# Score products of an attention block on row groups of 32: one head per group, both stacks double buffered

## The reference

```
a   = layernorm(x) @ w_attn + b_attn            # q, k, v; 16 heads of 8
s   = q @ k.T / sqrt(8) + slope[head] * key_position, causal
y   = softmax(s) @ v ;  x2 = x + y @ w_proj + b_proj
z   = layernorm(x2)
out = x2 + gate(z) * sum over 8 experts of (gelu(z @ w1 + b1) @ w2 + b2)
```

## Time and profile before

| | |
|---|---|
| median of three runs | 341.5 us |
| profiled execution, first to last instruction (span) | 341.4 us |
| PE busy | 295.9 us (87%), 1784 matrix instructions |
| PEld busy | 193.8 us (57%) |
| DVE busy | 192.6 us (56%) |
| ACT busy | 193.7 us (57%) |
| POOL busy | 84.1 us (25%) |
| chain that ended last, by engine | PE 74%, DVE 12%, DMA 7% |

### The profile page before, as it was taken

One profiled execution on the slowest core, in us unless ns is written; L12 is line 12 of the kernel. 1 busy time (PEld: TensorE's weight loads), 2 busy tenths in 40 slices (PEclk: granted clock), 3 DMA queues, 4 the chain that ended last, 5 costly groups with the idle time before them and its releaser, 6 DMA issues.

```text
span 341.4 us, 5507 instructions
## 1 busy us (share of the span) xinstructions
PE 295.9 (87%) x1784; PEld 193.8 (57%) x1784; DVE 192.6 (56%) x787; ACT 193.7 (57%) x322; POOL 84.1 (25%) x213
## 2 busy tenths in 40 slices
PE   0245899997979999699999997899999999998994
PEld 0133466565556676466766765557756665655661
DVE  5624759776786867145677776264867741161111
ACT  1871064463455568275759467376667788634462
POOL 8569203240233027002033126002210220000030
PEclk9985579999999999699999999899999999999999
DMA  7166500070120006200300028001100100000101
GB/s 198 66 90 96 193 2 2 16 122 9 38 74 4 0 19 105 29 2 18 95 1 4 0 61 120 3 2 44 35 4 2 35 2 2 0 2 0 31 1 31
DMA packets 12380, 13.29 MB, mean 39 GB/s; under 512 B 2048, under 2 KB 9088, under 8 KB 12096
## 3 DMA queue, kind: packets, MB, share of 16 engines
q1 hardware_dynamic: 11328, 11.90, 16.1%
q0 software_dynamic: 1024, 1.05, 1.9%
HBM read 5.21 MB, written 1.05 MB: 18 GB/s over the span
## 4 chain that ended last, share of the span: by engine, by line
PE 74%; DVE 12%; DMA 7%; issue 3%; ACT 1%; POOL 1%; DVEq 0%; SPq 0%; ACTq 0%; POOLq 0%
PE ffn_bank L835 16%; PE a_ring L742 11%; PE v_ring L720 11%; PE pv_bank L767 9%; DMA k_stack<-k_lo 6%; PE a_ring L673 5%; DVE unused L1047 5%; PE a_ring L748 5%; PE a_ring L674 4%; PE a_ring L675 4%; DVE xn L967 2%; PE v_ring L796 1%; PE v_ring L729 1%; DMA x_in<-x 1%; PE v_ring L673 1%
## 5 line engine op out<-in xcount | busy, mean ns | idle before, releaser
L1047 DVE CUSTOM_DVE_ANT_0 unused<-v_ring,cst 128x512 bf16<-128x512 f32 (+3 forms) x256 | 112.1, 487 | 68.5 <-PE v_ring L720 63.9
L553 ACT ACTIVATE probs<-a_ring 128x512 f32<-128x512 f32 (+1 forms) x192 | 92.5, 526 | 74.7 <-PE a_ring L748 73.5
L720 PE MATMUL v_ring<-k_stack,q_stack 128*128 128x512 f32 (+3 forms) x256 | 89.6, 422 | 20.2 <-DMA k_stack<-k_lo 15.3
L742 PE MATMUL a_ring<-q_stack,k_stack 128*128 128x512 f32 (+3 forms) x256 | 76.8, 360 | 0.4 <-DMA q_stack<-m_lo 0.4
L720 PEld LDWEIGHTS v_ring<-k_stack,q_stack 128*128 128x128 f32 x256 | 49.5, 210 | 40.6 <-issue 23.5
L570 ACT ACTIVATE hidden<-a_ring,cols_sb 128x512 f32<-128x512 f32 x64 | 43.4, 688 | 43.2 <-PE a_ring L675 42.7
L835 PE MATMUL ffn_bank<-hidden,w_sb 128*128 128x512 f32 x128 | 66.3, 602 | 1.1 <-ACT ffn_T L579 0.8
L742 PEld LDWEIGHTS a_ring<-q_stack,k_stack 128*128 128x128 f32 x256 | 46.7, 197 | 7.8 <-issue 4.0
L748 PE MATMUL a_ring<-score_mask,ident_bf 128*128 128x128 bf16 (+1 forms) x192 | 48.1, 252 | 0.0
L767 PE MATMUL pv_bank<-probs,v_ones 128*32 128x256 f32 (+3 forms) x512 | 43.2, 447 | 0.0
L673 PE MATMUL a_ring<-zT_hi,w_hi 128*128 128x512 f32 x64 | 34.2, 534 | 0.8 <-DVEq L953 0.8
(11 more groups left out here) (109 smaller groups left out, 298.4 us busy)
## 6 DMA issues: line engine op xcount, KB each, us to landing
q_stack<-q_hi SPq DMA_DIRECT2D x8, 256.0 KB
k_stack<-k_hi SPq DMA_DIRECT2D x64, 32.0 KB
x_in<-x SPq DMA_DIRECT2D x4, 256.0 KB, 3.6
hidden<-w SPq DMA_DIRECT2D x1, 1024.0 KB, 8.3
q_stack<-q_lo SPq DMA_DIRECT2D x4, 256.0 KB
k_stack<-k_lo POOLq DMA_DIRECT2D x32, 32.0 KB, 4.0
w_sb<-w SPq DMA_DIRECT2D x1, 1024.0 KB, 5.2
x_res<-x SPq DMA_DIRECT2D x4, 256.0 KB, 3.1
```

Of the source, the lines that this page charges most:

```text
L553: act.activation(probs[:, n % 2, q, KIND_AT[kind]:KIND_AT[kind] + cols], a_bank()[:, 0:cols], ACT.Exp).then_inc(e_freed, 1)
L720: last = pe.matmul(dst[:, at:at + P * (n + 1)], q_stack[b % 2][:, s, n * P:(n + 1) * P], k_stack[:, s, q, 0:P * (n + 1)], start=True, stop ...
L742: pe.matmul(dst[:, at:at + P * (TB - j)], k_stack[:, s, q, j * P:(j + 1) * P], q_stack[b % 2][:, s, j * P:T], start=(at == 0), stop=False, ...
L1047: ins = dve.tensor_tensor_reduce(unused[:, (uses[0] - 1) % V_BANKS, at:at + cols], bank_[:, at:at + cols], cst[:, C_MASK + T - cols:C_MASK ...
```

## The change

Each head gets 32 rows of its own, `QR * q` to `QR * q + 31`, in both stacks: 8 rows of q high (or k high), 8 of q low (k high), 8 of q high (k low), then two slope rows (24, 25), two maxima rows (26, 27), four unused. `k_stack` has no copies by head any more and is double buffered as `q_stack` is. A max unit reads 26 rows and an exp unit 28 rows at partition 32 q. The fill with zeros, the transfer of zeros, and POOL's transfers go away. Max units now go kind by kind like exp units, and exp units start with head 2, so that heads of neighbouring units differ. All loads of q and k are transfers of 64 KB from 32 partitions to 8, twelve for q and twelve for k per batch, issued by SP, for batch 0 the k ones by ACT. The mask product is unchanged.

```
+HEAD_D = 8
+ALIBI_ROWS, MAX_ROWS, STACK_ROWS = 24, 26, 28
...
-        k_stack = sb("k_stack", [P, SETS, QUADS, T], F32R)
+        k_stack = [sb(f"k_stack{i}", [P, SETS, T], F32R) for i in range(2)]
...
+        def send_term(queue, stack, term, part, loaded):
+            for q in range(QUADS):
+                row = QR * q + HEAD_D * term
+                queue.dma_start(stack[row:row + HEAD_D, :, :].bitcast(F32),
+                                part[QR * q:QR * (q + 1), :].bitcast(F32)).then_inc(loaded, 16)
+        def send_q(queue, b):
+            if b < 2:
+                queue.wait_ge(q_const, SETS * (b + 1))
+            else:
+                queue.wait_ge(e_filled, UNITS * SETS * (b - 1))
+            queue.wait_ge(q_split, 2 * b + 1)
+            send_term(queue, q_stack[b % 2], 0, q_hi, q_loaded)
+            send_term(queue, q_stack[b % 2], 2, q_hi, q_loaded)
+            queue.wait_ge(q_split, 2 * b + 2)
+            send_term(queue, q_stack[b % 2], 1, q_lo, q_loaded)
+        def send_k(queue, b):          # the same with k_const, k_split, k_hi (terms 0, 1), k_lo (term 2)
...
+        def exp_order(k):
+            return k // QUADS, (k + QUADS // 2) % QUADS
...
                     if s == 2 and b + 1 < B:
-                        load_k(b + 1, 0)
-                        load_q(b + 1)
+                        send_k(sp, b + 1)
+                        send_q(sp, b + 1)
...
-            pool.memset(k_stack[0:CONST_ROWS, 0:2, :, :].bitcast(F32), 0.0).then_inc(k_zeros, 1)
-            pool.memset(k_stack[0:CONST_ROWS, 2:4, :, :].bitcast(F32), 0.0).then_inc(k_zeros, 1)
-            load_k_low(0, 0)
-            load_k_low(0, 1)
...
             q_constants(0)
             k_constants(0)
             split_high(0, 1)
             split_high(0, 0)
+            send_k(act, 0)
             k_constants(1)
...
-                q, kind = k // KINDS, k % KINDS
+                kind, q = k // QUADS, k % QUADS
+                rows = slice(QR * q, QR * q + MAX_ROWS)
...
-                    last = pe.matmul(dst[:, at:at + P * (n + 1)], q_stack[b % 2][:, s, n * P:(n + 1) * P],
-                                     k_stack[:, s, q, 0:P * (n + 1)], start=True, stop=True)
+                    last = pe.matmul(dst[:, at:at + P * (n + 1)], q_stack[b % 2][rows, s, n * P:(n + 1) * P],
+                                     k_stack[b % 2][rows, s, 0:P * (n + 1)], start=True, stop=True)
...
+                rows = slice(QR * q, QR * q + STACK_ROWS)
-                    pe.matmul(dst[:, at:at + P * (TB - j)], k_stack[:, s, q, j * P:(j + 1) * P],
-                              q_stack[b % 2][:, s, j * P:T], start=(at == 0), stop=False, skip_group_check=True)
+                    pe.matmul(dst[:, at:at + P * (TB - j)], k_stack[b % 2][rows, s, j * P:(j + 1) * P],
+                              q_stack[b % 2][rows, s, j * P:T], start=(at == 0), stop=False, skip_group_check=True)
```

More of the change, by code:

```diff
@@ L38 @@
 QR = P // QUADS
-TERMS = 3
 MASKED = -3.0e38
@@ L319, in chunk @@
             return n // SETS, range(first, first + sizes[n % SETS])
[L321 to L325, removed]
+        def send_term(queue, stack, term, part, loaded):
[14 more added lines that the diff above has]
+        def send_k(queue, b):
+            if b < 2:
+                queue.wait_ge(k_const, SETS * (b + 1))
+            else:
+                queue.wait_ge(e_filled, UNITS * SETS * (b - 1))
+            queue.wait_ge(k_split, 2 * b + 1)
+            send_term(queue, k_stack[b % 2], 0, k_hi, k_loaded)
+            send_term(queue, k_stack[b % 2], 1, k_hi, k_loaded)
+            queue.wait_ge(k_split, 2 * b + 2)
+            send_term(queue, k_stack[b % 2], 2, k_lo, k_loaded)
+        def exp_order(k):
+            return k // QUADS, (k + QUADS // 2) % QUADS
         def inverse_sqrt(engine, settle, y, src, scale, eps, v, t, fused=False):
@@ L356, in load_residual @@
                 sp.dma_start(x_res[:], x_view[b]).then_inc(xres_loaded, 16)
[L358 to L380, removed]
             def load_max(b, s):
                 sp.wait_ge(m_ready, SETS * b + s + 1)
[L384 to L385 removed]
+                for r, part in ((MAX_ROWS, m_hi), (MAX_ROWS + 1, m_lo)):
+                    sp.dma_start(q_stack[b % 2][r::QR, s, :].bitcast(F32),
                                  part[:].bitcast(F32)).then_inc(m_loaded, 16)
@@ L433, in split_low @@
             def split_low(b, part):
-                full, hi, lo, parts, loads, count = (
-                    (k_full, k_hi, k_lo, k_split, k_low_loaded[0] + k_low_loaded[1], K_LOW_LOADS * b),
-                    (q_full, q_hi, q_lo, q_split, [q_loaded], q_count(b)))[part]
+                full, hi, lo, parts, loaded = ((k_full, k_hi, k_lo, k_split, k_loaded),
+                                               (q_full, q_hi, q_lo, q_split, q_loaded))[part]
                 pool.wait_ge(parts, 2 * b + 1)
                 if b >= 1:
-                    for loaded in loads:
-                        pool.wait_ge(loaded, count)
+                    pool.wait_ge(loaded, STACK_LOADS * b)
                 pool.tensor_tensor(lo[:], full[:], hi[:].bitcast(F32), ALU.subtract).then_inc(parts, 1)
@@ L447, in set_ones @@
                 pool.memset(slots[:, :, :, 16 + 8 * e:24 + 8 * e], 1.0).then_inc(v_const, 1)
-            def load_k_low(b, half):
-                if b == 0:
-                    pool.wait_ge(k_zeros, half + 1)
-                else:
-                    pool.wait_ge(e_filled, UNITS * (SETS * (b - 1) + 2 * half + 2))
-                pool.wait_ge(k_split, 2 * b + 2)
-                for q in range(QUADS):
-                    send_k(pool, k_lo, half, 1, q, k_low_loaded[half][q])
             steps = [0]
@@ L585, in split_high @@
             def split_high(b, part):
-                full, hi, ready, parts, loads, count = (
-                    (k_full, k_hi, k_ready, k_split, k_loaded[0] + k_loaded[1], K_LOADS * b),
-                    (q_full, q_hi, q_ready, q_split, [q_loaded], q_count(b)))[part]
+                full, hi, ready, parts, loaded = ((k_full, k_hi, k_ready, k_split, k_loaded),
+                                                  (q_full, q_hi, q_ready, q_split, q_loaded))[part]
                 act.wait_ge(ready, b + 1)
                 if b >= 1:
-                    for loaded in loads:
-                        act.wait_ge(loaded, count)
+                    act.wait_ge(loaded, STACK_LOADS * b)
                 act.activation(hi[:], full[:], ACT.Copy).then_inc(parts, 1)
```

77 lines of the change are left out of this document (28 added, 49 removed).

## The result

The changed kernel takes 433.1 us (median of five runs, 431.2 to 438.1) beside 341.5 (339.8 to 343.9) for the kernel before: a ratio of 1.267, 95% interval 1.260 to 1.275. The profiled execution is the longest of the five (438.1; the others had 431.2 to 433.2); its span of 436.3 us stands against 341.4.

The account below looks back on a forecast made before the run. It took PE's stream of products plus four waits for loads as the bound; 341.4 + 45 (stream) + 5 (start) - 3 (borders) = 388 us, range 338 to 400, likeliest case alone 378 to 400.

Parts of the forecast that it names:

- the granted clock falls: Rival on PE: emptier stretches bring its clock to 1.2 GHz for a good part, over 400 us; chance 0.04.
- Passing, forecast +3.0 a set: PE's stream: 13 tiled stretches per set pay for switching to and from whole-array products, 48 us for 16 sets.
- The price at pv: Read at the column-tiled pv products on PE: some 0.10 us in, 0.10 out, then first weights unhidden.
- The overlap: PE products of different heads running at the same time; alone, with free passing, worth 1.07 us per set, 17 in all.
- The first cycle: PE: max 384 + 128, exp 512, mask 128 take 0.81 us instead of 0.64, four times a set.
- the second pair: PE: max 256, exp 384 + 128, mask 256 take 0.77 us instead of 0.48, three times a set.
- The seven pairs: PE, per set: four max-exp pairs at +0.17 to +0.18 us each and three at +0.28.
- the other stretches: PE's remaining tiled stretches per set, exp units alone or other unit groupings, each +0.11 to +0.29 us.
- The upper bound of the stream, +65: PE's stream with the column form's passing price and no overlap: 48 + 17 = 65 us.
- The start, forecast +5: First max unit waits for all 24 transfers, landing at 34.5 us instead of 29.59; bounds +3 and +15.
- the bound made from it, 44: Start: at 0.25 us a packet the first loads would land at 44 us, the +15 bound.
- The borders, forecast -3: PE's load waits before set 3 at three batch borders: 4.3 and twice 0.7 us, against 2.8 + 3.1 + 3.2.

Follow-up runs that it names:

- spread: Changed kernel with its 24 transfers of 64 KB per batch going to 32 partitions instead of 8 (rows misplaced, for times only): 397.6 us, 1.159.
- loads_rows64: Kernel before with q and k loads reordered, max and exp products on rows 0 to 63 for every head (for times only): 425.2 us, 1.239.

## Why the prediction was wrong

The direction was right, and passing between tiled and whole-array products does cost time, as forecast. The time was 45 us over the forecast and 33 over the top of the range. The step that failed is the clock, which the sum left at nothing: it stood apart as the rival "the granted clock falls" with a chance of 0.04, where it was the largest term. The prices of the start and of the borders were too small as well; the price of the stream at full clock was too large, which hid part of it.

**The clock, forecast at nothing.** 40 to 50 us. It was set apart as a rival of its own, as if it excluded the forecast; it came on top of it. It was also looked for in the wrong place: "if emptier stretches bring it to its lower level". The stretches at the lower level are not empty (53.00 busy of 53.00 in spread). The row that was quoted, 0.82 from 40 to 60 us, comes from early sets that are score products nearly alone, with PE busy 18.92 of 20; there the clock had not fallen but not yet risen from the wait for the first loads (up at 47.1, PE at work from 29.59). The change takes four fifths of the rows from just those products, and what this does to the clock was never asked.

**Passing, forecast +3.0 a set: +1.8 measured, 29 us instead of 48.** The price at pv holds: 0.10 in and 0.10 out, against 0.22 for a tiled mask. Without overlap the prediction's own terms give 3.0 + 1.07 = 4.1, and loads_rows64 has 3.7. The overlap was taken too small. The first cycle was forecast at 0.81 us and takes 0.60. That a weight load does not wait for the other row group's is the likely reason. PE's weight loads after:

```profile
320.34 0.18 PEld L686 LDWEIGHTS v_ring<-k_stack,q_stack 26*128 26x128 f32 x1
320.34 0.29 PEld L709 LDWEIGHTS a_ring<-q_stack,k_stack 28*128 28x128 f32 x2
```

Two loads start together, where the prediction took them one after another at 0.107. For the second pair it forecast 0.77, and 0.64 is measured. The seven pairs were forecast at +1.5 a set and cost +0.3, which is the whole difference; the other stretches were forecast at +1.4 and cost some +1.5. The upper bound of the stream, +65, left the clock out and was passed (70.5).

**The start, forecast +5: +15.6.** The number of engines, eight, was right. The packet's price was not: 0.14 came from transfers that trickled at 40 GB/s, each alone, and 0.20 to 0.28 is paid when eight engines are full. The 0.25 of the earlier trace rows was nearer, and the bound made from it, 44, was missed by 1.

**The borders, forecast -3: +8.8.** SP's chain of 16.8 us was right (17.2). That the data land 1.9 us behind it was wrong, by the same price: the 22 to 28 us of the transfers, not the issues, end last. The 4 us forecast for the first border were met (4.1) by luck: the transfers took 3 us longer than forecast (21.8 against 16.8 + 1.9), and PE, at the lower clock, came later too; the 0.7 forecast for the others became 4.7 and 9.1. With slower sets the chain alone would have cost nothing (spread).

**What was named to show it.** Mask to next max unit 0.15 or more: 0.16. Starts within 0.02 us: 0.01. Exp product to mask 0.1 longer than the columns say: the mask starts 0.43 us after the product of 512 columns (319.75 to 320.18), 0.11 more than 0.21 for them and 0.11 for its weights. PE has no gap of 1 us from set 4 on but for two borders. "Wrong if the distance from one mask to the next stays at 0.6 us" came half true: in the first pair it is 0.60 at 2.4 GHz and 0.95 at 1.2. At full clock this pair loses nothing by the change; the second pair and the shorter stretches do.

## What to carry to other kernels

Products on fewer rows took as long as before, so tiling by rows can pay only where different row groups run together; here even with every score and mask product tiled the overlap did no more than pay for the passages. A whole-array product between tiled ones costs some 0.2 us each time. Where a change thins what the array does in stretches that are already near the lower clock, price the stretch at that level too and add it to the forecast instead of setting it beside. Take a transfer's packet price from a row with as many engines busy as the new transfers will have, and count the destination's partitions: here the same bytes to 8 instead of 32 took 0.20 to 0.28 us a packet instead of 0.13, on half the engines. A change of order alone, in the old kernel, gave 12.5 us.

## Not expected of the hardware

- A PE that the profile shows busy for 53.00 of 53.00 us was granted 0.50 of its clock, in a stretch of score products on 26 and 28 rows (spread); in the same kernel 24.00 of 24.00 us had 1.00. After the change the clock fell at 183.6 us, behind 12.00 busy us of 12.00.
- Weight loads for different row groups start within 0.01 us of each other (both at 320.34), as the products do (319.74 and 319.75).
- A 2 KB packet to 8 partitions takes 0.28 us with eight engines full (61 GB/s together) and 0.20 in another stretch of the same kernel (87 GB/s), to 32 partitions 0.13 with sixteen (203 GB/s).
- Whole-array products on 72 rows keep the pace of 128 at the upper clock (18.8 us a set against 18.7), those on 64 take 22.2 to 22.4: tiling begins between the two, not with the first unused row.
